# Spatial gate of a small convolutional transformer with its pixels on partitions, gates by tanh, and three tail products

## The chip, the cores and the metric

The kernel runs on one core of one Trainium2 chip. The metric is the device time of one execution in microseconds (us). Three executions of the kernel before took 211.3, 211.53 and 212.07 us; the median is 211.53 us. Engines are called PE (TensorE; PEld are its weight loads), DVE (VectorE), ACT (ScalarE), POOL (GpSimd) and SP (SyncE).

## What is computed

The input is x, float32, 4 images of 64 channels and 16 x 16 pixels. Four layers each add a mixer and then a mixture of eight experts. The change touches the mixer of layer 1 alone. Its reference, cut to what matters (`out` is the sum of a 1x1, a 3x3 and a 5x5 convolution of the normalised input):

```python
avg = jnp.mean(out, axis=(2, 3), keepdims=True)
mx = jnp.max(out, axis=(2, 3), keepdims=True)
ca = jax.nn.sigmoid(ca_mlp(avg) + ca_mlp(mx))                 # one gate per image and channel
c = out * ca
sa_in = jnp.concatenate([jnp.mean(c, axis=1, keepdims=True), jnp.max(c, axis=1, keepdims=True)], axis=1)
sa = jax.nn.sigmoid(conv2d(sa_in, sa_w, pad=3))               # one gate per image and pixel, 7x7
cbam_out = c * sa
...
similarity = jnp.exp(-dist_sq / (2.0 * sigma * sigma))
attn = jax.nn.softmax(similarity, axis=-1)
ao = jnp.einsum('bnm,bcm->bnc', attn, v)
non_local = out + ao.reshape(B, C, H, W)
cat = jnp.concatenate([cbam_out, non_local], axis=1)
return conv2d(cat, tail_w, tail_b)                            # 1x1, 128 -> 64 channels
```

## The kernel before

All data stay in SBUF. A tile has 128 partitions: two images of 64 channels one above the other (`HALVES`), and 512 columns: two parts (`INNER`, the index `j`) of 256 pixels. `chunk(t, j)` is the part j, `tile(t, i)` a piece of 128 columns. Nothing is scheduled by a program: every engine has its own block, the order in it is written out by hand, and the engines wait for each other by semaphores (`S[...]`). PE executes its products in the order of its block.

The mixer of layer 1 on PE (from L531): 25 taps of the convolution (L555) for part 0, then 25 for part 1. Between the taps of part 1 stand the small works of part 0: `queries_keys` (L443), `channel_hidden` and `channel_gates` (L450, L457, the channel gate), `values` (L462), `gated_tokens` (L484: the gated image is transposed, so that a pixel is a partition), `distances` (L472), `spatial_gates` (L490). Behind the taps the same works follow for part 1 (L559 to L574), mixed with `attend` (L508), `spatial_map` (L502), `tail` (L523) and `center` (L293) of the next layer norm. The two engines beside it:

- DVE (L1197 to L1210): `gate_channels(j)` prepares the queries and keys and multiplies by the channel gate; `token_features(j)` (L1164) takes the sum and the maximum over the channels of each pixel, from PSUM; `gate_logits(j)` (L1174) clamps the logits of the pixel gate; `gate_both` (L1179) multiplies by the pixel gate; `normalise` (L1183) divides the attention by its sum and adds the convolution's output `O`; `add_input` (L1192) adds the bias and the layer's input.
- ACT (L814 to L831): for each part it copies the convolution's output, squares queries and keys, applies the exponentials of the attention (`similarities`, L793) and of the gates. A sigmoid is written with Exp, Ln and Exp over a tile of two partitions (one per image) and 256 pixels (`gate_pixels`, L806).

The pixel gate is a product of the features (weights of two columns) with a Toeplitz matrix of the 7x7 kernel (256 moving columns), four times (L497). Its result has an image per partition, and `spatial_map` spreads it to 128 partitions by a product with `to_half`. These are its lines:

```python
last = mm(gate_ps[j][0:2, 0:PIX], sa_feat[:, at:at + 2],
          toeplitz[:, (2 * c + n) * PIX:(2 * c + n + 1) * PIX], ...)
```

Of the kernel before, what the change touches and what calls it, by code (L numbers as in the profile page):

```python
# [27 lines left out]
def pack_plan():  # L28

    plan = {  # L30
        "first": [("center", 128), ("average", 128), ("eps6", 1), ("eps5", 1), ("minus_one", 1), ("one", 1)],
# [21 lines left out]
def metaformer(nc, a):  # L53
# [7 lines left out]
    with ExitStack() as ctx:  # L61
# [24 lines left out]
        to_half = sb("to_half", [2, 128])  # L86
# [24 lines left out]
        def tile(t, i):  # L111
# [4 lines left out]
            borders_zero c_tok ca_cl ca_e ca_h ca_in ca_r ca_s ca_top cbam_done conv_done conv_loaded  # L116
# [7 lines left out]
            route_parts routed route_rows route_shift route_transposed sa_bc sa_cl sa_in sa_map sa_ps small_loaded  # L124
# [37 lines left out]
        O, QK, gated, cbam, ao_n, nonlocal_ = mixer  # L162
# [28 lines left out]
        ca = sb("ca", [128, 4 * INNER])  # L191
        sa = sb("sa", [2, 4 * COLS])
# [30 lines left out]
        SETUP = 8  # L223

# [58 lines left out]
        def _(pe):  # L283
# [173 lines left out]
            def channel_gates(j):  # L457
                pe.wait_ge(S["small_loaded"], 64)
                pe.wait_ge(S["ca_r"], j + 1)
                mm(gate_ps[j][:, 0:1], ca2[0:8, :], ca_in[:, j:j + 1], start=True, stop=True).then_inc(S["ca_s"], 1)  # L460
# [11 lines left out]
            def distances(j):  # L472

                pe.wait_ge(S["qk_lin"], 4 * j + 4)
                pe.wait_ge(S["qk_sq"], 4 * j + 4)
                pe.wait_ge(S["pool_setup"], SETUP)
                for h in range(HALVES):
                    for m in range(2):
# [1126 lines left out]
```

## Time and profile before

| | |
|---|---|
| median of three executions | 211.53 us |
| the profiled execution's own time | 211.5 us |
| its span, first to last instruction | 209.7 us |
| PE busy | 195.9 us (93%), 1112 records |
| DVE busy | 124.5 us (59%) |
| ACT busy | 129.3 us (62%) |
| POOL busy | 42.5 us (20%) |
| granted clock of PE, mean | 1.000 |
| share of the chain that ended last, PE | 78% |

Busy times are sums of the records of an engine; they overlap between engines. An f32 product shows two records on PE and two on PEld. The chain that ended last is followed back from the last instruction, at each step to what released it. The gap between the span and the execution's own time (1.8 us) lies outside of the instructions.

### The profile page before, as it was taken

What the parts mean: (1) busy time and instruction counts of PE and PEld (TensorE: products, weight loads), DVE (VectorE), ACT (ScalarE), POOL (GpSimd) and SP (SyncE); (2) the same over time, 40 slices, a digit from 0 to 9 for tenths busy, and PEclk for the clock granted to TensorE, in tenths of its full rate; (3) what the DMA queues carried; (4) which work ended last, traced back from release to release, by engine and by line L of the source; (5) the groups of instructions that cost most, each with busy time, mean ns of one, the idle gap of its engine ahead of it and who ended that gap; (6) DMA issues with size and microseconds to landing.
All of it is one profiled execution on the core that took longest, in us unless ns stands there. A gap on an engine that the chain in (4) does not pass through costs nothing.

```text
span 209.7 us, 3083 instructions
## 1 busy us (share of the span) xinstructions
PE 195.9 (93%) x1112; PEld 91.5 (44%) x1120; DVE 124.5 (59%) x364; ACT 129.3 (62%) x216; POOL 42.5 (20%) x60
## 2 busy tenths in 40 slices
PE   7998999999999998999999999999998997799993
PEld 2654222348876764322222363532234594333221
DVE  0466879957641824945342547595455688586435
ACT  2535688646355683776575830688685675598682
POOL 7761000000000000103963000100920011010740
PEclk9999999999999999999999999999999999999999
DMA  6999300000000000000000000000000000000001
GB/s 228 355 407 404 123 0 2 0 0 3 2 3 0 3 0 0 0 5 0 0 0 0 0 3 0 0 0 0 0 6 0 2 0 3 0 0 0 3 0 50
DMA packets 3119, 8.40 MB, mean 40 GB/s; under 512 B 550, under 2 KB 1072, under 8 KB 2976
## 3 DMA queue, kind: packets, MB, share of 16 engines
q1 hardware_dynamic: 2736, 7.60, 9.7%
q0 software_dynamic: 224, 0.46, 0.6%
q8 instruction: 9, 0.15, 0.3%
q10 hardware_dynamic: 144, 0.13, 0.2%
q14 instruction: 6, 0.05, 0.1%
HBM read 7.94 MB, written 0.26 MB: 39 GB/s over the span
## 4 chain that ended last, share of the span: by engine, by line
PE 78%; DVE 10%; ACT 8%; issue 3%; DVEq 0%; ACTq 0%
PE bank L362 17%; PE banks L379 9%; PE banks L291 8%; PE banks L380 7%; PE banks L555 6%; PE bank L302 5%; PE bank L296 4%; ACT hidden L727 3%; PE bank L343 3%; PE banks L516 2%; PE banks L497 2%; PE bank L612 2%; PE bank L480 2%; PE bank L325 2%; ACT rstd L689 1%
## 5 line engine op out<-in xcount | busy, mean ns | idle before, releaser
L727 ACT ACTIVATE hidden<-banks,pack_l 128x1024 f32<-128x1024 f32 (+1 forms) x43 | 44.9, 1052 | 18.3 <-PE banks L380 17.8
L362 PE MATMUL bank<-hidden,w 128*64 128x512 f32 (+1 forms) x160 | 41.4, 596 | 1.3 <-ACT hidden L727 1.3
L291 PE MATMUL banks<-idle_work 128*128 128x512 bf16 x116 | 31.1, 401 | 2.0 <-DVE idle_work L1000 1.2
L379 PE MATMUL banks<-split_x,w_hi 128*128 128x512 f16 x80 | 30.7, 384 | 0.0
L380 PE MATMUL banks<-split_x,w_lo 128*128 128x512 f16 x80 | 30.3, 379 | 0.0
L1442 POOL CAST split_x<-normed 64x256 f16<-64x256 f32 x8 | 4.0, 494 | 99.7 <-DVE normed L896 95.2
L685 ACT ACTIVATE squares<-bank 128x256 f32<-128x256 f32 x18 | 6.9, 383 | 22.5 <-PE bank L296 22.4
L379 PEld LDWEIGHTS banks<-split_x,w_hi 128*128 128x128 f16 x80 | 7.7, 97 | 28.4 <-issue 11.5
L291 PEld LDWEIGHTS banks<-idle_work 128*128 128x128 bf16 x123 | 12.4, 105 | 16.2 <-issue 5.0
L1451 POOL TENSOR_TENSOR total<-total,term 128x512 f32<-128x512 f32 x12 | 17.6, 1463 | 2.6 <-DVE term L982 2.0
L362 PEld LDWEIGHTS bank<-hidden,w 128*64 128x64 f32 x160 | 7.9, 134 | 18.3 <-issue 13.6
L896 DVE TENSOR_TENSOR normed<-bank,rstd 128x256 f32<-128x256 f32 x16 | 6.7, 424 | 12.8 <-ACT rstd L689 12.7
L982 DVE TENSOR_TENSOR term<-relu_sim,bank 128x512 f32<-128x512 f32 x12 | 7.8, 685 | 9.5 <-PE bank L343 6.1
L555 PE MATMUL banks<-padded,conv_hi 128*64 128x256 f16 x100 | 12.0, 280 | 0.1
L555 PE MATMUL banks<-padded,conv_lo 128*64 128x256 f16 x100 | 11.9, 277 | 0.0
L302 PE MATMUL bank<-squares,pack_first 128*128 128x256 f32 x36 | 11.3, 414 | 0.4
L736 ACT ACTIVATE relu_sim<-bank,pack_l 128x512 f32<-128x512 f32 x16 | 10.9, 682 | 1.0 <-PE bank L362 0.8
L982 DVE TENSOR_TENSOR term<-sq_sim,bank 128x512 f32<-128x512 f32 x6 | 4.1, 687 | 11.9 <-ACT sq_sim L736 6.8
L296 PE MATMUL bank<-x,pack_first 128*128 128x256 f32 x28 | 9.1, 419 | 1.7 <-DVE x L998 0.7
L1451 POOL TENSOR_TENSOR total<-x,term 128x512 f32<-128x512 f32 x3 | 3.8, 1270 | 33.3 <-DVE term L982 33.3
L689 ACT ACTIVATE rstd<-bank,pack_first 128x256 f32<-128x256 f32 x18 | 8.3, 472 | 3.1 <-PE bank L302 2.8
L380 PEld LDWEIGHTS banks<-split_x,w_lo 128*128 128x128 f16 x80 | 7.8, 98 | 4.7
(314 smaller groups left out, 322.3 us busy)
## 6 DMA issues: line engine op xcount, KB each, us to landing
w_stage<-in_w SPq DMA_DIRECT2D x3, 512.0 KB, 13.2
w_stage<-in_w SPq DMA_DIRECT2D x1, 1024.0 KB, 9.6
conv<-in_conv SPq DMA_DIRECT2D x1, 800.0 KB, 7.7
w<-in_w SPq DMA_DIRECT2D x3, 256.0 KB, 13.4
w<-in_w SPq DMA_DIRECT2D x1, 512.0 KB, 10.4
toeplitz<-in_toeplitz SPq DMA_DIRECT2D x1, 512.0 KB, 11.2
gauss<-in_gauss SPq DMA_DIRECT2D x1, 512.0 KB, 12.4
pack_l<-in_pack_l SPq DMA_DIRECT2D x1, 373.5 KB, 14.9
```

Source lines behind the costliest of these rows:

```text
L291: mm(out, idle_work[:, 0:128], idle_work[:, 0:cols], start=True, stop=True)
L296: mm(bank[4 + j][:, 0:PIX], P("first", "center"), chunk(src, j), start=True, stop=True)\
L302: mm(bank[6 + j][:, 0:PIX], P("first", "average"), chunk(squares, j), start=True, stop=True)\
L362: last = mm(out[64 * h:64 * h + 64, cut], w2[l][:, (f * NE + e) * CH:(f * NE + e + 1) * CH], hidden[v % 3][:, h * 512 + cut.start:h * 512 ...
L379: mm(out, w1_hi[l][:, at:at + 128], split_x[h][:, :], start=True, stop=False)
L380: last = mm(out, w1_lo[l][:, at:at + 128], split_x[h][:, :], start=False, stop=True)
L555: last = mm(image(conv_ps[j][64 * h:64 * h + 64, 0:PIX]), w[:, t * CH:(t + 1) * CH], pads[h][:, j, dy:dy + SIDE, dx:dx + SIDE], start=t == ...
L689: act(chunk(rstd, j), bank[6 + j][:, 0:PIX], ACT.Abs_reciprocal_sqrt, bias=P("first", "eps6" if LN_EPS[k] == 1e-6 else "eps5")).then_inc(S ...
L727: last = act(hidden[u % 3][:, cut], both[u % 2][:, cut], ACT.Gelu, bias=P(f"l{l}", "e_b1")[:, e * fc + f:e * fc + f + 1])
L736: act(y_sb[e], bank[4 + e % 2][:, :], ACT.Identity, bias=P(f"l{l}", "e_b2")[:, e:e + 1])\
L982: TT(out[:, :], y_sb[e], bank[6 + e % 2][:, :], ALU.mult).then_inc(S["moe_term"], 1)
L1451: G.tensor_tensor(total[:, :], (total if e else x[2 * l + 1])[:, :], term[e % 3][:, :], ALU.add)\
```

## The change

It does these things, all in the mixer of layer 1:

- The product of the pixel gate is turned: the Toeplitz matrix gives the weights (128 x 128) and the features are the moving operand (two columns), eight times per part. The logits then have a pixel per partition, 128 x 4 in all.
- The mean over the channels comes from PE: `gated_tokens` gets a product with a column of `average` beside each transpose; the DVE copies four columns instead of summing and scaling.
- Both sigmoids are written as 0.5 tanh(x/2) + 0.5, with one ACT pass (on 128 x 1 and on 128 x 4); the DVE's clamps go. `widen_gates` writes each pixel's gate 64 times, and `spatial_map` transposes this with two products with the identity. The set of ACT's tables that is loaded ahead is another one.
- `normalise` no longer adds `O`; the tail has a third product, of `tail1` with `O`.
- The order: `distances` ahead of `gated_tokens` (and with a wait per image), `values(1)` ahead of `channel_hidden(1)`, `attend(1)` and `spatial_map(1)` ahead of `tail(0)`, `center(4, 0)` directly behind `tail(0)`; on the DVE `token_features(1)` behind `gate_both(0)` and `normalise(0)`, and `add_input(0)` behind `gate_both(1)`.
- The constants `to_half` and `one` go, with the DMA of `to_half`.

```diff
             def gated_tokens(j):
                 pe.wait_ge(S["gated_c"], j + 1)
                 for m in range(2):
-                    last = tr(tile(gate_ps[j], m), tile(gated, 2 * j + m), P("l0", "identity"))
+                    tr(tile(gate_ps[j], m), tile(gated, 2 * j + m), P("l0", "identity"))
+                    last = mm(gate_ps[j][:, MEANS + 2 * m:MEANS + 2 * m + 2], tile(gated, 2 * j + m),
+                              P("first", "average")[:, 0:65:64], start=True, stop=True)
                 last.then_inc(S["c_tok"], 1)
 
             def spatial_gates(j):
                 pe.wait_ge(S["toeplitz_loaded"], 16)
                 pe.wait_ge(S["sa_in"], 2 * j + 2)
-                for c in range(2):
-                    for n in range(2):
-                        at = 8 * j + 4 * c + 2 * n
-                        last = mm(gate_ps[j][0:2, 0:PIX], sa_feat[:, at:at + 2],
-                                  toeplitz[:, (2 * c + n) * PIX:(2 * c + n + 1) * PIX],
-                                  start=c + n == 0, stop=c + n == 2)
+                for o in range(2):
+                    for c in range(2):
+                        for n in range(2):
+                            at, to = 8 * j + 4 * c + 2 * n, (2 * c + n) * PIX + o * 128
+                            last = mm(gate_ps[j][:, LOGITS + 2 * o:LOGITS + 2 * o + 2], toeplitz[:, to:to + 128],
+                                      sa_feat[:, at:at + 2], start=c + n == 0, stop=c + n == 2)
                 last.then_inc(S["sa_ps"], 1)
 
             def spatial_map(j):
-                pe.wait_ge(S["sa_map"], j + 1)
-                mm(gate_ps[j][:, 0:PIX], to_half[:, :], sa[:, 4 * PIX * j + 3 * PIX:4 * PIX * (j + 1)],
-                   start=True, stop=True).then_inc(S["sa_bc"], 1)
+                pe.wait_ge(S["sa_wide"], j + 1)
+                for o in range(2):
+                    last = mm(tile(gate_ps[j], o), tile(sa_wide, 2 * j + o), P("l0", "identity"), start=True, stop=True)
+                last.then_inc(S["sa_bc"], 1)
...
-                pairs = [("tail0", "cbam_done", cbam), ("tail1", "nonlocal_in", nonlocal_)]
-                for n, (weight, ready, src) in enumerate(pairs if j == 0 else pairs[::-1]):
+                parts_ = [("tail1", "conv_out", O), ("tail0", "cbam_done", cbam), ("tail1", "nonlocal_in", ao_n)]
+                for n, (weight, ready, src) in enumerate(parts_):
                     pe.wait_ge(S[ready], j + 1)
-                    last = mm(tail_ps[j][:, 0:PIX], P("l1", weight), chunk(src, j), start=n == 0, stop=n == 1)
+                    last = mm(tail_ps[j][:, 0:PIX], P("l1", weight), chunk(src, j), start=n == 0, stop=n == 2)
...
             queries_keys(1)
+            values(1)
             channel_hidden(1)
             spatial_map(0)
             channel_gates(1)
             attend(0, range(2, 4))
-            values(1)
+            distances(1)
             gated_tokens(1)
-            distances(1)
             spatial_gates(1)
+            attend(1)
+            spatial_map(1)
             tail(0)
-            attend(1)
             center(4, 0, x[3], x_ready(3))
-            spatial_map(1)
             tail(1)
...
             def gate_pixels(j):
-                part = [sa[:, (4 * j + n) * PIX:(4 * j + n + 1) * PIX] for n in range(4)]
-                sc.wait_ge(S["sa_cl"], j + 1)
-                st.link(act(part[1], part[0], ACT.Exp, scale=-1.0))
-                st.link(act(part[2], part[1], ACT.Ln, bias=P("first", "one")[0:2, :]))
-                act(part[3], part[2], ACT.Exp, scale=-1.0).then_inc(S["sa_map"], 1)
+                sc.wait_ge(S["sa_ps"], j + 1)
+                tanh_half(sa_tanh[:, 4 * j:4 * j + 4], gate_ps[j][:, LOGITS:LOGITS + 4]).then_inc(S["sa_map"], 1)
...
                 by_group = gate_ps[j][:, 0:PIX].rearrange("p (g c) -> p g c", c=64)
-                summed = st.mark(rsum(sa_feat[:, 8 * j:8 * j + 4], by_group))
+                V.tensor_copy(sa_feat[:, 8 * j:8 * j + 4], gate_ps[j][:, MEANS:MEANS + 4]).then_inc(S["sa_in"], 1)
                 rmax(sa_feat[:, 8 * j + 4:8 * j + 8], by_group).then_inc(S["sa_in"], 1)
-                ve.wait_ge(st.sem, summed)
-                TS(sa_feat[:, 8 * j:8 * j + 4], sa_feat[:, 8 * j:8 * j + 4], 1.0 / CH, None, ALU.mult)\
-                    .then_inc(S["sa_in"], 1)
...
+            def widen_gates(j):
+                ve.wait_ge(S["sa_map"], j + 1)
+                TS(chunk(sa_wide, j).rearrange("p (g c) -> p g c", c=64), spread_to(sa_tanh[:, 4 * j:4 * j + 4], 64),
+                   0.5, 0.5, ALU.mult, ALU.add).then_inc(S["sa_wide"], 1)
...
-                st.link(TT(chunk(ao_n, j).rearrange("p (r c) -> p r c", c=64), got[:, :, 0:64], spread_to(iz, 64),
-                           ALU.mult))
-                TT(chunk(nonlocal_, j), chunk(ao_n, j), chunk(O, j), ALU.add).then_inc(S["nonlocal_in"], 1)
+                TT(chunk(ao_n, j).rearrange("p (r c) -> p r c", c=64), got[:, :, 0:64], spread_to(iz, 64), ALU.mult)\
+                    .then_inc(S["nonlocal_in"], 1)
```

How the order moves, at three places. First PE behind the second half of attention 0, that is the distances, the transposes and the pixel gate of part 1. `mixer` stands for `O`, `gated`, `cbam` and the like, `R` and `L` are the operands of the distances, `banks` are PSUM. Before:

```order
L469 MATMUL banks<-pack_l,mixer 128x128 [waits v_rows]
L469 MATMUL banks<-pack_l,mixer 128x128
L487 MATMUL banks<-pack_l,mixer 128x128 [waits gated_c]
L487 MATMUL banks<-pack_l,mixer 128x128
L480 MATMUL bank<-R,L 128x256 [waits pool_setup,qk_sq,qk_lin]
L480 MATMUL bank<-R,L 128x256 x3
L497 MATMUL banks<-toeplitz,sa_feat 2x256 [waits sa_in,toeplitz_loaded]
L497 MATMUL banks<-toeplitz,sa_feat 2x256 x3
```

After the change:

```order
L481 MATMUL bank<-R,L 128x256 [waits qk_sq,qk_lin,pool_setup]
L481 MATMUL bank<-R,L 128x256
L481 MATMUL bank<-R,L 128x256 [waits qk_sq,qk_lin]
L481 MATMUL bank<-R,L 128x256
L489 MATMUL banks<-pack_l,mixer 128x128 [waits gated_c]
L490 MATMUL banks<-pack_first,mixer 128x2
L489 MATMUL banks<-pack_l,mixer 128x128
L490 MATMUL banks<-pack_first,mixer 128x2
L502 MATMUL banks<-sa_feat,toeplitz 128x2 [waits sa_in,toeplitz_loaded]
L502 MATMUL banks<-sa_feat,toeplitz 128x2 x7
```

The distances stand ahead of the transposes now, the values have gone to an earlier place, two products of two columns came in, and the gates follow the transposes directly.

Second, PE from there to the last `center` of the stage (L296, L297 in the changed kernel). Before:

```order
L528 MATMUL banks<-mixer,pack_l 128x256 [waits cbam_done]
L528 MATMUL banks<-mixer,pack_l 128x256 [waits nonlocal_in]
L516 MATMUL banks<-v_rows,sq_sim 64x65 [waits attn,v_rows]
L516 MATMUL banks<-v_rows,sq_sim 64x65 x15
L296 MATMUL bank<-x,pack_first 128x256 [waits x_ready]
L505 MATMUL banks<-sa,to_half 128x256 [waits sa_map]
L528 MATMUL bank<-mixer,pack_l 128x256 [waits nonlocal_in]
L528 MATMUL bank<-mixer,pack_l 128x256 [waits cbam_done]
L296 MATMUL bank<-x,pack_first 128x256 [waits x_ready]
```

After the change:

```order
L521 MATMUL banks<-v_rows,sq_sim 64x65 [waits attn,v_rows]
L521 MATMUL banks<-v_rows,sq_sim 64x65 x15
L510 MATMUL banks<-pack_l,mixer 128x128 [waits sa_wide]
L510 MATMUL banks<-pack_l,mixer 128x128
L533 MATMUL banks<-mixer,pack_l 128x256 [waits conv_out]
L533 MATMUL banks<-mixer,pack_l 128x256 [waits cbam_done]
L533 MATMUL banks<-mixer,pack_l 128x256 [waits nonlocal_in]
L297 MATMUL bank<-x,pack_first 128x256 [waits x_ready]
L533 MATMUL bank<-mixer,pack_l 128x256 [waits conv_out]
L533 MATMUL bank<-mixer,pack_l 128x256 [waits cbam_done]
L533 MATMUL bank<-mixer,pack_l 128x256 [waits nonlocal_in]
L297 MATMUL bank<-x,pack_first 128x256 [waits x_ready]
```

Attention 1 and the map of the pixel gate went ahead of both tails; a center stands directly behind the tail that it waits for, and the second tail behind that center.

Third, the DVE from the value rows of part 1 (L1160, L1157) to the first addition of the input (L1194, L1187). Before:

```order
L1160 TENSOR_TENSOR v_rows<-banks,pack_l 128x4x64 [waits v_rows_ps]
L892 TENSOR_REDUCE sa_feat<-banks 128x4 [waits c_tok]
L889 TENSOR_REDUCE sa_feat<-banks 128x4
L1171 TENSOR_SCALAR sa_feat<-sa_feat 128x4 [waits dve_chain]
L1181 TENSOR_TENSOR mixer<-banks,mixer 128x256 [waits sa_bc]
L1187 RECIPROCAL inv_z<-banks 128x4 [waits ao_ps]
L1188 TENSOR_TENSOR mixer<-banks,inv_z 128x256 [waits dve_chain]
L1190 TENSOR_TENSOR mixer<-mixer 128x256 [waits dve_chain]
L1176 TENSOR_SCALAR sa<-banks 2x256 [waits sa_ps]
L1194 SCALAR_TENSOR_TENSOR x<-banks,pack_l,x 128x256 [waits tail]
```

After the change:

```order
L1157 TENSOR_TENSOR v_rows<-banks,pack_l 128x4x64 [waits v_rows_ps]
L1175 TENSOR_TENSOR mixer<-banks,mixer 128x256 [waits sa_bc]
L1181 RECIPROCAL inv_z<-banks 128x4 [waits ao_ps]
L1182 TENSOR_TENSOR mixer<-banks,inv_z 128x256 [waits dve_chain]
L1165 COPY sa_feat<-banks 128x4 [waits c_tok]
L890 TENSOR_REDUCE sa_feat<-banks 128x4
L1170 TENSOR_SCALAR mixer<-sa_tanh 128x256 [waits sa_map]
L1181 RECIPROCAL inv_z<-banks 128x4 [waits ao_ps]
L1182 TENSOR_TENSOR mixer<-banks,inv_z 128x256 [waits dve_chain]
L1175 TENSOR_TENSOR mixer<-banks,mixer 128x256 [waits sa_bc]
L1187 SCALAR_TENSOR_TENSOR x<-banks,pack_l,x 128x256 [waits tail]
```

The features of part 1 (from `c_tok`) come behind the gate and the attention of part 0, and the input is added last.

## Rows read from the trace of the kernel before

**Rows 1.** The page, its span and first part, and the cores' granted clock

```profile
span 209.7 us, 3083 instructions
PE 195.9 (93%) x1112; PEld 91.5 (44%) x1120; DVE 124.5 (59%) x364; ACT 129.3 (62%) x216; POOL 42.5 (20%) x60
core 0: 209.7 us, clock 1.000
```

**Rows 2.** Busy time by stretch, from the last tap to the end of the tails

```profile
66.50:72.80 6.30, 6.30 (x60) 4.96 (x56) 4.58 (x19) 3.67 (x10) 0.00 (x0) 1.00 0.00 0
72.80:80.30 7.50, 7.50 (x53) 4.46 (x52) 2.89 (x8) 4.93 (x9) 0.00 (x0) 1.00 0.01 2
```

Columns: stretch, its length, then busy us and records of PE, PEld, DVE, ACT and POOL, granted clock, DMA share, GB/s.

**Rows 3.** Timeline of PE: start, us from start to end, line, operands, idle before

```profile
70.73 0.44 PE L487 MATMUL banks<-pack_l,mixer 128*128 128x128 f32 x2
...
74.64 1.13 PE L528 MATMUL banks<-mixer,pack_l 128*128 128x256 f32 x4
75.70 2.14 PE L516 MATMUL banks<-v_rows,sq_sim 128*64 128x65 f32 x32
77.77 0.70 PE L296 MATMUL bank<-x,pack_first 128*128 128x256 f32 x2
78.40 0.69 PE L505 MATMUL banks<-sa,to_half 2*128 2x256 f32 x2
79.04 1.27 PE L528 MATMUL bank<-mixer,pack_l 128*128 128x256 f32 x4
80.89 0.70 PE L296 MATMUL bank<-x,pack_first 128*128 128x256 f32 x2 [0.58 <-DVE x L1194]
```

**Rows 4.** Timeline of ACT, exponentials of attention 1 and gate of part 1

```profile
73.52 1.32 ACT L804 ACTIVATE sq_sim<-relu_sim,pack_first 128x512 f32<-128x512 f32 x2
75.20 0.42 ACT L810 ACTIVATE sa<-sa 2x256 f32<-2x256 f32 x1 [0.36 <-DVE sa L1176]
...
76.19 0.42 ACT L812 ACTIVATE sa<-sa 2x256 f32<-2x256 f32 x1
```

**Rows 5.** Timeline of PE's weight loads behind the last tap

```profile
67.38 0.23 PEld L447 LDWEIGHTS bank<-mixer,pack_l 128*64 128x64 f32 x4
67.99 0.10 PEld L454 LDWEIGHTS banks<-stats,pack_l 128*8 128x8 f32 x2 [0.39 <-DVE stats L1140]
...
70.89 1.60 PEld L480 LDWEIGHTS bank<-R,L 96*128 96x128 f32 x8
72.82 1.38 PEld L497 LDWEIGHTS banks<-toeplitz,sa_feat 128*2 128x2 f32 x8 [0.33 <-issue]
74.64 0.73 PEld L528 LDWEIGHTS banks<-mixer,pack_l 128*128 128x128 f32 x4 [0.44 <-issue]
...
79.04 0.30 PEld L528 LDWEIGHTS bank<-mixer,pack_l 128*128 128x128 f32 x2 [0.35 <-DVE mixer L1190]
79.61 0.30 PEld L528 LDWEIGHTS bank<-mixer,pack_l 128*128 128x128 f32 x2 [0.27 <-DVE mixer L1181]
```

**Rows 6.** Weight loads and small products of other shapes: timeline, and single lines (ns min/median/max)

```profile
83.78 0.97 PEld L325 LDWEIGHTS bank<-pack_l,normed 128*128 128x128 f32 x8 [0.66 <-DVE normed L896]
...
L325 PEld LDWEIGHTS bank<-pack_l,normed x24: 186/192/192, 83.8 to 185.3; 128*128 128x128 f32 x24
...
75.70 2.00 PEld L516 LDWEIGHTS banks<-v_rows,sq_sim 128*64 128x64 f32 x32 [0.33 <-issue]
...
L593 PE MATMUL bank<-bn,pack_l x2: 251/262/272, 129.8 to 129.9; 128*128 128x2 f32 x2
```

**Rows 7.** Timeline of DVE: features of part 1, and the last addition

```profile
71.20 0.42 DVE L892 TENSOR_REDUCE sa_feat<-banks 128x4 f32<-128x256 f32 x1
71.54 0.41 DVE L889 TENSOR_REDUCE sa_feat<-banks 128x4 f32<-128x256 f32 x1
71.88 0.16 DVE L1171 TENSOR_SCALAR sa_feat<-sa_feat 128x4 f32<-128x4 f32 x1
...
80.35 0.48 DVE L1194 SCALAR_TENSOR_TENSOR x<-bank,pack_l,x 128x256 f32<-128x256 f32 x1 [0.79 <-PE bank L528]
```

More of the change, by code:

```diff
@@ L30, in pack_plan @@
     plan = {
-        "first": [("center", 128), ("average", 128), ("eps6", 1), ("eps5", 1), ("minus_one", 1), ("one", 1)],
+        "first": [("center", 128), ("average", 128), ("eps6", 1), ("eps5", 1), ("minus_one", 1)],
         "l0": [("identity", 128), ("W", 128), ("b_row", 64), ("router", 16), ("router_b", 8), ("e_b1", 8),
@@ L161, in metaformer @@
         qnorm, rnorm, unit, t_rows = mixer[0:4]
-        O, QK, gated, cbam, ao_n, nonlocal_ = mixer
+        O, QK, gated, cbam, ao_n, sa_wide = mixer
         upsampled, bn_in, bn_relu = mixer[0:3]
@@ L190, in metaformer @@
         ca_in = sb("ca_in", [8, 2])
-        ca = sb("ca", [128, 4 * INNER])
-        sa = sb("sa", [2, 4 * COLS])
+        ca = sb("ca", [128, 2 * INNER])
+        sa_tanh = sb("sa_tanh", [128, 4 * INNER])
         sa_feat = sb("sa_feat", [128, 16])
@@ L223, in metaformer @@
         SETUP = 8
+        MEANS, LOGITS = 256, 264
         ROOTS, LOGS = "abs_reciprocal_sqrt_and_small", "natural_log_exp_and_others"
@@ L457, in channel_gates @@
             def channel_gates(j):
-                pe.wait_ge(S["small_loaded"], 64)
+                pe.wait_ge(S["small_loaded"], 48)
                 pe.wait_ge(S["ca_r"], j + 1)
@@ L547, in _ @@
                         if t == 13:
+                            distances(0)
                             gated_tokens(0)
-                            distances(0)
                         if t == 17:
@@ L1136, in gate_channels @@
                 mean, top = stats[:, 2 * j:2 * j + 1], stats[:, 2 * j + 1:2 * j + 2]
-                gate = [ca[:, 4 * j + n:4 * j + n + 1] for n in range(4)]
                 ve.wait_ge(S["conv_out"], j + 1)
@@ L1149, in gate_channels @@
                         .then_inc(S["qk_lin"], 1)
-                    if h == 0:
-                        ve.wait_ge(S["ca_s"], j + 1)
-                        TS(gate[0], gate_ps[j][:, 0:1], -80.0, None, ALU.max).then_inc(S["ca_cl"], 1)
                 ve.wait_ge(S["ca_e"], j + 1)
-                st.link(TS(gate[2], gate[1], 1.0, None, ALU.add))
-                st.link(V.reciprocal(gate[3], gate[2]))
-                TS(chunk(gated, j), chunk(O, j), gate[3], None, ALU.mult).then_inc(S["gated_c"], 1)
+                tanh, gate = ca[:, 2 * j:2 * j + 1], ca[:, 2 * j + 1:2 * j + 2]
+                st.link(TS(gate, tanh, 0.5, 0.5, ALU.mult, ALU.add))
+                TS(chunk(gated, j), chunk(O, j), gate, None, ALU.mult).then_inc(S["gated_c"], 1)
             def value_rows(j):
@@ L1199, in _ @@
             token_features(0)
-            gate_logits(0)
+            widen_gates(0)
             gate_channels(1)
             value_rows(1)
-            token_features(1)
             gate_both(0)
             normalise(0)
-            gate_logits(1)
-            add_input(0)
+            token_features(1)
+            widen_gates(1)
             normalise(1)
             gate_both(1)
+            add_input(0)
             add_input(1)
@@ L1532 @@
     vals["first"] = {"center": eye - avg, "average": avg, "eps6": np.full((128, 1), 1e-6), "eps5": np.full((128, 1), 1e-5),
-                     "minus_one": np.full((128, 1), -1.0), "one": np.ones((128, 1))}
+                     "minus_one": np.full((128, 1), -1.0)}
     vals["l0"] = {"identity": eye, "W": _both_halves(v["L0_conv_W"].T), "b_row": _row(v["L0_conv_b"]),
```

22 lines of the change are left out of this document (7 added, 15 removed).

## The prediction

> **What bounds the kernel now.** I read the page first: one core, TensorE busy 93% of 209.7 us, its granted clock 1.000 (the 2.4 GHz level) throughout [rows 1]. The other engines have room, so the question is whether TensorE leads in the stage that changes too. The busy time by stretch answers it: between 66.5 us and 80.3 us, the part of the layer-1 mixer behind the convolutions, PE is busy for all of 6.30 and of 7.50 us, while VectorE and ScalarE are busy for 4.58 and 3.67 us, then for 2.89 and 4.93 us [rows 2]. TensorE runs in program order, so a product queued ahead of the last `center(4, 1)` moves everything behind it.
>
> The timeline of PE at the end of the stage has hardly a hole: gates of the pixels (L497), tail 0, attention 1, `center(4, 0)`, pixel map 1, tail 1; only then 0.58 us idle until VectorE has added the input, and `center(4, 1)` starts at 80.89 us [rows 3]. ScalarE's chain for the pixel gate of batch part 1 ends at 76.19 + 0.42 = 76.61 us [rows 4], and PE takes its result (L505) only at 78.40 us [rows 3]. That chain, which the change shortens, is 1.8 us off the path. What the change adds to PE is on it.
>
> **How PE spends a group.** The weight loads show the pace [rows 5]. Four f32 products with 256 moving columns take 72.82 - 70.89 = 1.93 us (L480), two take 75.70 - 74.64 = 1.06 us [rows 3], one takes 78.40 - 77.77 = 0.63 us [rows 3]: 0.43 us for each further product, 0.63 us for the last of a group. Each f32 product is two records. With 128 weight columns and few moving ones (L325, 16 columns) eight loads take 0.97 us, each lasting 0.19: (0.97 - 0.19) / 7 = 0.111 us from one record to the next [rows 6]. That is the price of the new small products.
>
> **The change, part by part.**
>
> 1. `gated_tokens` gets two products for the channel means beside its two transposes: 2 x 2 records x 0.111 = 0.44 us. It runs for both batch parts, on PE, nothing beside it: **+0.88**. VectorE loses a sum of 0.42 us and a scaling of 0.16 us and gains a small copy, which PE doesn't see for part 0 (four taps of the convolution stand between).
>
> 2. `spatial_gates` now loads the Toeplitz blocks as weights and moves two columns: 8 products, 16 records x 0.111 = 1.78 us, against 74.64 - 72.82 = 1.82 us now (L497) [rows 5]. **0**. I take the row of L325 because its weights have the same shape; both bounds stand in the rivals.
>
> 3. `spatial_map` becomes two products of 128 columns (4 records, 0.44 us and the end of a group) for one of 256 (0.63 us): **0**.
>
> 4. `tail` gets a third product, 0.43 us, in both parts: **+0.86**. The sum on VectorE that it replaces (0.42 us each) isn't on PE's path: in tail 0 it was long done, in tail 1 part of a wait, see 7.
>
> 5. New wait, `spatial_gates(1)`: before, `distances(1)` (1.93 us) stood between the transposes and the gates and covered VectorE's reductions. Now `distances(1)` comes ahead of the transposes and nothing is between. A small product lasts 0.262 us (L593) [rows 6], 0.15 more than the 0.111 to the next record; then 0.03 to VectorE's start (71.17 to 71.20), 0.16 for the copy (nearest row L1171), 0.41 for the maximum [rows 7], 0.06 back to PE (80.83 to 80.89): **+0.81**. Behind it are queued attention 1 and both tails. The cover that moved doesn't help anyone: attention 1 waits for ScalarE's exponentials, whose 1.32 us end at 74.84 [rows 4], before PE asks for them either way.
>
> 6. New wait, `center(4, 0)`: now attention 1 stands between tail 0 and this center. In the new order tail 0 is directly ahead of it, and tail 1 is queued behind. The last rows of the stage show the price: load of the last tail product 79.61, VectorE's addition 80.35 to 80.83, center 80.89 [rows 3, 5, 7], 1.28 us from load to load where an unhindered group takes 0.63: **+0.65**.
>
> 7. Given back: the small product of the channel gate waits for VectorE's mean (load at 67.99, 0.61 us behind the last, where 0.45 is the pace of that group) [rows 5]; now `values(1)` fills it: **-0.15**. Tail 1's second product comes 79.61 - 79.04 = 0.57 us after the first because of the pixel gate's product on VectorE [rows 5]; that is done early now: 0.43, **-0.14**.
>
> 8. The three ScalarE passes for the pixel gate (0.42 each or more) [rows 4] become one small tanh, VectorE's clamps go, one tiny DMA goes, and the table load of the stage is exchanged for one of another set. None of it is on the path, for PE asks later: **0**. If PE did wait there, this would be worth 1.1 us per part (third rival).
>
> Sum: 0.88 + 0.86 + 0.81 + 0.65 - 0.29 = **+2.9 us**. The profiled execution took 211.5 us (span 209.7), the median is 211.53, so the two stand together and the sum carries over: **214.4 us**, 1.4% more. The layers behind are unchanged and only shift. About 0.5% (1.06 us) is what a measurement here can tell from no change.
>
> **Rivals.**
>
> *Cheap weight loads.* The 40 records of the small products (32 in the gates, 8 for the means) could cost less than 0.111 us, if the next load runs fully under the product before it. For it: attention's loads of 64 columns follow each other in (2.00 - 0.217) / 31 = 0.0575 us [rows 3, 5, 6]. Against it: L325 has the very shape and shows 0.111. At 0.0575 the sum loses 40 x 0.0535 = 2.1 us: 212.3. At nothing at all it loses 4.4: 210.0. So it ends between faster and the same. Its point of decision is the record pitch of the gates' products: below some 0.063 us the change reads as none.
> The Trainium skill ("TensorE: Matmul & The Clock Gate", section "Back-to-back issue gap") has a table by which a product with up to 64 moving columns follows in about 60 cycles; at 2.4 GHz that would make 1.0 us of the 40 records, an estimate, and 211.0 us of the whole. By the row of L325 the table doesn't hold where every product brings new f32 weights.
>
> *Products that accumulate wait for each other.* The gates' eight products add into the same two columns. If each of the 32 records had to end (0.262 us) before the next, that is 32 x 0.151 = 4.8 us more: 219.2. No row shows so small an accumulating product; L497's, 256 wide, don't wait.
>
> *The pixel gate's chain is the bound after all.* Then taking two ScalarE passes and the clamp out saves some 1.1 us per part and the added products run under other waits: 211.5 - 2.2 = 209.3, **faster**. It decides only if the map of part 1 were ready after 78.40 us; it is ready at 76.61 [rows 3, 4].
>
> *The two new waits cost little,* because PE preloads weights and VectorE answers faster than its rows: without 5 and 6 the time is 213.0, still slower. PE can't go around a waiting product, which speaks against it.
>
> **How the numbers follow.** The forecast as summed 0.71; cheap loads 0.12 (0.03 of it faster, 0.09 the same); accumulation 0.04; chain as the bound 0.03; cheap waits 0.10. The forecast's own lower tail gives 0.02 to "the same". Faster 0.03 + 0.03 = 0.06; the same 0.11; slower 0.69 + 0.04 + 0.10 = 0.83. The range leaves out the accumulation above and most of the first and third rival below: 212.3 (the loads at 0.0575) to 216.0 (each of the four terms a third to a half larger: 2.9 x 1.5 = 4.4). The forecast's own range is 213.4 to 215.6.
>
> **What would show it.** In the profile after: the gates' eight products in about 1.8 us; two small ones of 0.44 us beside the transposes; three tail products in 1.5 us; PE idle by some 0.8 us ahead of the gates of part 1, released by VectorE's maximum, and by some 0.6 us ahead of `center(4, 0)`; `center(4, 1)` at about 83.8 us in place of 80.89, and the same distance from there to the end. It is wrong if that start comes before 82, if the gates take under 1 us or over 3, or if PE waits for the wide gates.

## The result, and the profile after

The changed kernel takes 215.08 us (median of four executions, 214.51 to 216.01) against 211.42 us for the kernel before beside it (211.07 to 212.07): the ratio is 1.0177, 95% interval 1.015 to 1.0203. It is slower by 3.7 us, where the prediction said 2.9 (214.4 us, range 212.3 to 216.0). The profiled execution took 214.51 us.

The first lines of its page, which answer to [rows 1], with the granted clock of the 40 slices of the span:

```profile
span 212.7 us, 3144 instructions
PE 198.6 (93%) x1152; PEld 97.1 (46%) x1152; DVE 122.2 (57%) x356; ACT 126.9 (60%) x212; POOL 42.0 (20%) x59
PEclk9999999999999969999999999999999999999999
```

DVE and ACT each lost 2.3 to 2.4 us of work, PE gained 2.7, and the time followed PE. What is new is in the third line: one slice at 0.6. The kernel before had the clock at its upper level all through.

The timeline of PE in the last part of the stage, which answers to [rows 3]:

```profile
68.69 0.71 PE L510 MATMUL banks<-pack_l,mixer 128*128 128x128 f32 x4
...
72.58 0.27 PE L489 MATMUL banks<-pack_l,mixer 128*128 128x128 f32 x1
72.69 0.28 PE L490 MATMUL banks<-pack_first,mixer 128*128 128x2 f32 x2
72.83 0.31 PE L489 MATMUL banks<-pack_l,mixer 128*128 128x128 f32 x1
72.97 0.28 PE L490 MATMUL banks<-pack_first,mixer 128*128 128x2 f32 x2
73.93 1.92 PE L502 MATMUL banks<-sa_feat,toeplitz 128*128 128x2 f32 x16 [0.68 <-DVE sa_feat L890]
75.78 2.19 PE L521 MATMUL banks<-v_rows,sq_sim 128*64 128x65 f32 x32
77.89 1.22 PE L510 MATMUL banks<-pack_l,mixer 128*128 128x128 f32 x4
78.91 1.87 PE L533 MATMUL banks<-mixer,pack_l 128*128 128x256 f32 x6
81.36 0.70 PE L297 MATMUL bank<-x,pack_first 128*128 128x256 f32 x2 [0.58 <-DVE x L1187]
81.89 1.46 PE L533 MATMUL bank<-mixer,pack_l 128*128 128x256 f32 x6
83.93 0.70 PE L297 MATMUL bank<-x,pack_first 128*128 128x256 f32 x2 [0.58 <-DVE x L1187]
```

Both new waits are there: 0.68 us ahead of the gates (L502), released by the maximum, and 0.58 us ahead of `center(4, 0)` (L297). Then compare like with like: the four records of L510 (map 1, two products) take 1.22 us; the same four for part 0, in the first line, take 0.71. The tail behind them, six records, lasts 1.87 us, the second tail with the same six lasts 1.46. The stretches of the stage say why (columns as in [rows 2]; the third from the right is the granted clock):

```profile
75.00:76.00 1.00, 1.00 (x12) 0.98 (x12) 0.00 (x0) 0.12 (x1) 0.00 (x0) 1.00 0.00 0
76.00:77.00 1.00, 1.00 (x20) 1.00 (x20) 0.29 (x1) 0.98 (x2) 0.00 (x0) 0.66 0.00 0
77.00:78.00 1.00, 1.00 (x18) 0.88 (x15) 0.00 (x0) 0.36 (x1) 0.00 (x0) 0.50 0.00 0
78.00:79.00 1.00, 1.00 (x5) 1.00 (x6) 0.61 (x2) 0.00 (x0) 0.00 (x0) 0.50 0.00 0
79.00:80.00 1.00, 1.00 (x5) 0.81 (x5) 0.42 (x1) 0.00 (x0) 0.00 (x0) 0.64 0.00 0
80.00:81.00 1.00, 0.78 (x4) 0.35 (x2) 0.18 (x1) 0.00 (x0) 0.00 (x0) 1.00 0.00 0
```

Between 76 and 80 us the clock goes down to its lower level, 1.2 GHz (0.50), and comes back. Before it fell, PE had waited, had run the 16 records of two columns and was in the attention. The busy share of PE doesn't show it: it is 1.00.

The weight loads, which answer to [rows 5]:

```profile
67.31 0.23 PEld L448 LDWEIGHTS bank<-mixer,pack_l 128*64 128x64 f32 x4
67.92 0.52 PEld L470 LDWEIGHTS banks<-pack_l,mixer 128*128 128x128 f32 x4 [0.39 <-issue]
...
72.83 0.34 PEld L490 LDWEIGHTS banks<-pack_first,mixer 128*128 128x128 f32 x2
73.90 1.86 PEld L502 LDWEIGHTS banks<-sa_feat,toeplitz 128*128 128x128 f32 x16 [0.73 <-issue]
75.78 2.00 PEld L521 LDWEIGHTS banks<-v_rows,sq_sim 128*64 128x64 f32 x32
```

(1.86 - 0.19) / 15 = 0.111 us per record: the pace that [rows 6] gave for another line. The gates take 75.78 - 73.90 = 1.88 us against 1.82 before (L497).

**The stage.** One number serves for all comparisons below: from the first weight load of `queries_keys(0)` to the first load of the last `center(4, 1)`. Before it is 80.89 - 55.33 = 25.56 us, after 83.93 - 54.86 = 29.07 us. The 3.51 us between them are nearly the whole 3.7 us; the stage merely began 0.47 us earlier in this execution. Each stage time below comes from one profiled execution, and the times in us are medians. The start of the stage lies between 54.58 and 55.84 us in the profiles of this document, whatever the kernel, so that the stage resolves more than the whole time does.

### The profile page after: what moved, and what is told of

It is laid out like the page before. It is cut to its first block, busy times and chain, and to the rows that moved or that the text cites. A ratio compares the mean times of both kernels' runs of the same rounds, so it can differ in the third digit from the quotient of the medians.

```text
span 212.7 us, 3144 instructions
## 1 busy us (share of the span) xinstructions
PE 198.6 (93%) x1152; PEld 97.1 (46%) x1152; DVE 122.2 (57%) x356; ACT 126.9 (60%) x212; POOL 42.0 (20%) x59
## 4 chain that ended last, share of the span: by engine, by line
PE 78%; DVE 11%; ACT 7%; issue 3%; DVEq 0%; ACTq 0%
PE bank L363 17%; PE banks L380 9%; PE banks L292 7%; PE banks L381 7%; PE banks L560 6%; PE bank L303 5%; PE bank L297 4%; ACT hidden L732 3%; PE bank L344 3%; PE banks L521 2%; PE bank L481 2%; PE banks L502 2%; PE bank L617 2%; PE bank L326 2%; ACT rstd L694 1%
## 5 line engine op out<-in xcount | busy, mean ns | idle before, releaser
L292 PE MATMUL banks<-idle_work 128*128 128x512 bf16 x123 | 32.0, 396 | 1.2 <-DVE idle_work L1001 1.2
L292 PEld LDWEIGHTS banks<-idle_work 128*128 128x128 bf16 x123 | 12.3, 105 | 16.0 <-issue 4.7
L297 PE MATMUL bank<-x,pack_first 128*128 128x256 f32 x28 | 9.1, 419 | 2.3 <-DVE x L1187 1.2
```

The costliest lines, as they stand in the source:

```text
L292: mm(out, idle_work[:, 0:128], idle_work[:, 0:cols], start=True, stop=True)
L297: mm(bank[4 + j][:, 0:PIX], P("first", "center"), chunk(src, j), start=True, stop=True)\
```

## The experiments

The theory was that waits and added products sum on PE, and, once the trace was seen, that the clock's fall adds to it. The questions: do the waits go when the order is repaired; what lets the clock fall; what is each part of the arithmetic worth.

**e1: the distances between the transposes and the gates.**

```diff
-            distances(1)
             gated_tokens(1)
+            distances(1)
             spatial_gates(1)
```

> The changed kernel with distances(1) back between gated_tokens(1) and spatial_gates(1), nothing else. 'Stage' is the time from the first weight load of queries_keys(0) to the first load of the last center(4, 1): 25.56 us before, 29.07 us after the change. Theory (waits and products add up, clock fell because PE was idle in the wait): the 0.68 us of idle time ahead of the gates of part 1 goes, and so does the stretch at a granted clock of 0.50: stage 27.6 to 27.8, about 1.4 us less than the changed kernel. Rival (the clock falls because the small products move two columns only, the wait has nothing to do with it): the wait goes, the stretch at 0.50 stays, stage 28.4, 0.7 us less. Second rival (the wait only moves, since the distances now delay the attention's exponentials): stage above 28.8.

Measured: 215.09 us, stage 84.49 - 55.31 = 29.18 us, nothing gained. Its timeline of PE, then its stretches:

```profile
73.76 1.84 PE L502 MATMUL banks<-sa_feat,toeplitz 128*128 128x2 f32 x16
76.01 2.19 PE L521 MATMUL banks<-v_rows,sq_sim 128*64 128x65 f32 x32 [0.41 <-ACT sq_sim L809]
78.13 1.22 PE L510 MATMUL banks<-pack_l,mixer 128*128 128x128 f32 x4
79.14 2.20 PE L533 MATMUL banks<-mixer,pack_l 128*128 128x256 f32 x6
```

```profile
77.00:78.00 1.00, 1.00 (x20) 1.00 (x18) 0.00 (x0) 0.23 (x1) 0.00 (x0) 0.61 0.00 0
78.00:79.00 1.00, 1.00 (x8) 0.88 (x6) 0.61 (x2) 0.00 (x0) 0.00 (x0) 0.50 0.00 0
```

The second rival holds: the wait ahead of the gates is gone (PE's loads wait 0.23 us for VectorE ahead of the transposes in its place), and the attention (L521) waits 0.41 us for ScalarE's exponentials instead, since the distances come later and tail 0 is no longer between. The clock falls all the same.

**e2: tail 0 ahead of attention 1.** The two lines of PE's order below, `spatial_map(1)` behind `center(4, 0)`, and `add_input(0)` ahead of `normalise(1)` on VectorE.

```diff
             spatial_gates(1)
+            tail(0)
             attend(1)
-            spatial_map(1)
-            tail(0)
             center(4, 0, x[3], x_ready(3))
+            spatial_map(1)
             tail(1)
```

> The changed kernel with tail(0) ahead of attend(1) and add_input(0) ahead of normalise(1) again, center(4, 0) and then spatial_map(1) behind attend(1); distances(1) stays ahead of gated_tokens(1). The wait of center(4, 0) goes (0.58 us of idle PE, 0.65 by the price of the prediction). Theory: stage 28.4 if the stretch at 0.50 stays. If the 256-wide products of tail 0 between the small products and the attention keep the clock up, another 0.7 less: 27.7. Rival (center(4, 0)'s wait was hidden): no change, 29.1.

Measured: 214.38 us, stage 83.81 - 55.41 = 28.40 us, 0.67 less than the changed kernel. The wait of `center(4, 0)` is gone, and the clock still falls:

```profile
78.00:79.00 1.00, 1.00 (x18) 1.00 (x18) 0.49 (x1) 0.00 (x0) 0.00 (x0) 0.50 0.00 0
```

The 0.67 us are near the price of that wait (0.65), but they are a net of several things: the low clock lies over the attention for the most part, which hardly feels it, and tail 1 now waits 0.48 us in its loads for VectorE's product with the gate. A cleaner reading of the same wait follows with e8.

**e3: both orders.**

> Both orders of the two runs before together: only the arithmetic of the change is left, in the old order apart from values(1) ahead of channel_hidden(1). Theory: both waits gone and the clock at 1.00: 29.07 - 0.7 - 0.65 - 0.7 = 27.0 for the stage; what is left over the kernel before, 1.4 to 1.6 us, is the 0.88 us of the mean products and the 0.86 us of the third tail products, less 0.15 to 0.3. Rival (the clock falls from the small products alone): 27.7. Rival (the added products are cheap and the waits were all of it): 25.6 to 26.

Measured: 213.30 us, stage 82.56 - 55.50 = 27.06 us, 2.0 less than the changed kernel. The timeline of PE has hardly any idle time but the last (the stretches have 0.09 us from 71 to 72 and 0.08 from 80 to 81):

```profile
73.95 1.84 PE L502 MATMUL banks<-sa_feat,toeplitz 128*128 128x2 f32 x16
75.65 1.54 PE L533 MATMUL banks<-mixer,pack_l 128*128 128x256 f32 x6
77.12 2.14 PE L521 MATMUL banks<-v_rows,sq_sim 128*64 128x65 f32 x32
79.19 0.70 PE L297 MATMUL bank<-x,pack_first 128*128 128x256 f32 x2
...
82.56 0.70 PE L297 MATMUL bank<-x,pack_first 128*128 128x256 f32 x2 [0.58 <-DVE x L1187]
```

The granted clock is 1.00 in every stretch of the stage. The order, with the fall of the clock that goes away with it, is worth 2.0 us of the 3.5; 1.5 us stay with the arithmetic.

**e4: the wait filled with products of zeros.**

```diff
             gated_tokens(1)
+            busy(3, bank[5][:, :])
             spatial_gates(1)
```

> The changed kernel with three products of zeros, 128 x 512 bf16 (0.22 us each by the rows of L291), ahead of spatial_gates(1), where PE waited for the features; no result depends on them. The wait stays in length, but PE is busy in it. Theory (the idle time made the clock fall): granted clock 1.00 throughout, stage 28.4, 0.7 us less than the changed kernel, though PE does more. Rival (the small products alone make it fall): the stretch at 0.50 stays, and the stage is 29.0 to 29.2. If the filling products run past the end of the wait, up to 0.2 us more in either case.

Measured: 215.37 us, stage 84.72 - 55.39 = 29.33 us. PE works through the wait (L292), and the clock falls none the less (0.69 from 77 to 78 us, 0.50 until 80):

```profile
73.64 0.81 PE L292 MATMUL bank<-idle_work 128*128 128x512 bf16 x3
...
79.44 2.13 PE L533 MATMUL banks<-mixer,pack_l 128*128 128x256 f32 x6
```

```profile
78.00:79.00 1.00, 1.00 (x12) 0.88 (x9) 0.43 (x2) 0.00 (x0) 0.00 (x0) 0.50 0.00 0
```

The idle time is not what it takes; the theory as I put it falls here, its rival holds. The filling is of zeros; whether other numbers would act alike is not shown.

**e8: the small products made wide.** The gates' products move 128 columns, the same two repeated, in the order and with the waits of the changed kernel.

```diff
-  last = mm(gate_ps[j][:, LOGITS + 2 * o:LOGITS + 2 * o + 2], toeplitz[:, to:to + 128],
-            sa_feat[:, at:at + 2], start=c + n == 0, stop=c + n == 2)
+  last = mm(gate_ps[j][:, MEANS + 128 * o:MEANS + 128 * o + 128], toeplitz[:, to:to + 128],
+            repeat(sa_feat[:, at:at + 2], 64), start=c + n == 0, stop=c + n == 2)
```

> The changed kernel, order and waits as they are, with each of the gates' small products moving 128 columns in place of 2 (the same two columns of features, repeated 64 times by the access pattern). The weight loads set their pace, 0.111 us a record, and a record of 128 moving columns takes no longer, so the gates still take 1.88 us. Theory (the clock falls because these products move almost nothing for 1.9 us, next to the wait and the attention): granted clock 1.00 throughout the stage, stage 28.4, 0.7 us less than the changed kernel, 214.4 us. Rival (the waits alone, or attention 1 alone, make it fall): the stretch at 0.50 stays, stage 29.1. Rival (the moving columns cost time of their own beside the loads): gates over 2.5 us each, stage over 29.5.

Measured: stage 83.94 - 55.59 = 28.35 us, 0.72 less than the changed kernel, clock 1.00 in all of it:

```profile
74.76 2.02 PE L502 MATMUL banks<-sa_feat,toeplitz 128*128 128x128 f32 x16 [0.68 <-DVE sa_feat L892]
76.72 2.14 PE L521 MATMUL banks<-v_rows,sq_sim 128*64 128x65 f32 x32
78.78 0.71 PE L510 MATMUL banks<-pack_l,mixer 128*128 128x128 f32 x4
79.33 1.46 PE L533 MATMUL banks<-mixer,pack_l 128*128 128x256 f32 x6
```

The same wait, the same attention, 64 times the moving columns, and the map and the tail are back at 0.71 and 1.46 us. Compare L510 to `center(4, 0)`: 81.37 - 78.78 = 2.59 us here, 81.36 - 77.89 = 3.47 us in the changed kernel. The low clock cost 0.88 us there; the slower gates (1.99 against 1.88 us, and 1.98 against 1.88 for part 0) took 0.2 back. This run also gives the wait of `center(4, 0)` at the upper clock: from the first load of tail 0 to the center 81.37 - 79.22 = 2.15 us, where e3, whose tail 0 has the attention behind it, takes 77.12 - 75.63 = 1.49: 0.66.

The whole time, though, was 215.52 us, no less than the changed kernel's: three of four executions had a mean clock of 0.992, as all four of the changed kernel have. In the profiled one the clock fell in layer 3, behind a stretch in which PE was busy for only 0.67 of 2 us:

```profile
181.00:183.00 2.00, 0.67 (x2) 0.30 (x2) 1.83 (x7) 1.76 (x2) 0.00 (x0) 1.00 0.00 0
183.00:185.00 2.00, 1.62 (x4) 1.00 (x4) 1.26 (x4) 0.00 (x0) 0.00 (x0) 0.64 0.00 0
185.00:187.00 2.00, 2.00 (x6) 1.37 (x6) 0.00 (x0) 0.77 (x2) 0.00 (x0) 0.51 0.00 0
```

That stretch is no reason by itself: the changed kernel has it too, with the same products and the same idle times ahead of them (0.78 and 0.98 us), and keeps its clock there:

```profile
181.00:183.00 2.00, 0.67 (x2) 0.30 (x2) 1.80 (x7) 1.72 (x2) 0.00 (x0) 1.00 0.00 0
183.00:185.00 2.00, 1.60 (x6) 0.89 (x6) 1.25 (x3) 0.38 (x1) 0.00 (x0) 1.00 0.00 0
```

From the last center to the end of the span e8 takes 213.8 - 83.94 = 129.9 us, the changed kernel 212.7 - 83.93 = 128.8: the fall there cost 1.1 us, more than the other one gave back. The one execution with a mean clock of 1.000 took 213.57 us. So two executions of e8 are known to have had no fall in the mixer; where the clock fell in the two others isn't known.

**e11: e1 with the wide products**, as a second test of the same cause in another order (the diffs of e1 and e8 together).

> e1_dist_between (stage 29.18 us, with a stretch at a granted clock of 0.50) with the gates' products moving 128 columns in place of 2, as in e8_wide_moving. Theory (the small products are what lets the clock fall): clock 1.00 in the mixer, stage 28.4 to 28.5, 0.7 us less than e1. Rival (e8's clock stayed up by chance, since the wait and the attention are as quiet as they were): the stretch at 0.50 is there again, stage 29.1 to 29.3.

Measured: stage 83.25 - 55.22 = 28.03 us, 1.15 less than e1, clock 1.00 in the mixer. More than expected, as e1's low clock lay over more of its tail (2.20 us against 1.46). The time was 214.89 us, again with a fall in layer 3 in the profile. Of the three other executions two had a mean clock of 0.992; one, at 0.998, took 214.67 us, no less than the rest.

**e5: two products in the tail**, on top of e3: VectorE adds `O` again.

```diff
-  parts_ = [("tail1", "conv_out", O), ("tail0", "cbam_done", cbam), ("tail1", "nonlocal_in", ao_n)]
+  parts_ = [("tail0", "cbam_done", cbam), ("tail1", "nonlocal_in", ao_n)]
...
+  TT(chunk(ao_n, j), chunk(ao_n, j), chunk(O, j), ALU.add).then_inc(S["nonlocal_in"], 1)
```

> e3_both (stage 27.06 us, 213.3 us) with the tail of two products again: VectorE adds the convolution's output in normalise as in the kernel before. Theory: 0.43 us of PE per part, stage 26.2 (0.86 less). Rival (the third product fills a wait, because the tail of part 1 waits for the pixel gate's product on VectorE between its second and third anyway, by 0.79 against 0.43 us): only the 0.43 us of part 0 come back and the addition of 0.42 us on VectorE delays that product, stage 26.6 to 27.0.

Measured: 213.11 us, stage 82.39 - 55.77 = 26.62 us, 0.44 less than e3: the rival. Only part 0 gives its 0.43 us back. In part 1 the tail waits for the pixel gate's product on VectorE, which now comes behind one more addition; PE's loads of that tail wait 0.70 us, and from the first load of map 1 to the last center both runs take 3.04 us.

**e6: sums over the channels on VectorE**, on top of e3: the two products with `average` go, the sum and the scaling come back.

> e3_both (stage 27.06 us, 213.3 us) without the mean products: VectorE sums over the channels and scales, as in the kernel before. Theory: each pair of small products costs 0.44 us of PE with nothing beside it, stage 26.2 (0.88 less); the features are ready in time, since distances(1) (1.9 us) covers VectorE's 0.9 us. Rival (small products cost less than the load pace says, since they run between the transposes): 0.5 us less or under, stage 26.5 to 26.9. In e3_both attention 1 also waited for ScalarE's exponentials by no more than 0.1 us; these start with the distances, which now come 0.44 us earlier, so that they don't bind.

Measured: 212.87 us, stage 82.31 - 55.84 = 26.47 us, 0.59 less. The transposes and the way to the distances take 0.17 us (71.58 to 71.75) where e3 took 0.56 (71.55 to 72.11): 0.39 us for the two small products of a part. With 0.34 for part 0 (below) that is 0.73, not 0.88, and some of it went into a short wait ahead of the gates (PE's loads pause 0.25 us), since VectorE's longer features come behind `gate_both(0)` and `normalise(0)`.

**e7: e5 and e6 together.**

> e5 and e6 together: of the change only the turned pixel gate, the tanh and values(1) ahead of channel_hidden(1) are left, in the order of the kernel before otherwise. Theory (the pixel gate with pixels on partitions costs PE nothing and gains nothing): stage 25.3 to 25.6 against 25.56 before, 211.2 to 211.5 us, no difference that can be told. Rival (the shorter chain of the gate is worth its 1.1 us per part): below 25.0 and below 210.5 us. Rival (the turned gate costs PE time of its own): above 25.9.

Measured: 213.74 us, stage 82.04 - 54.74 = 27.30 us: outside of the theory. The timeline of PE shows two waits and a low clock (1.22 us for L297):

```profile
70.76 1.89 PE L481 MATMUL bank<-R,L 96*128 96x256 f32 x8
72.99 1.92 PE L500 MATMUL banks<-sa_feat,toeplitz 128*128 128x2 f32 x16 [0.34 <-DVE sa_feat L1166]
...
77.93 1.22 PE L297 MATMUL bank<-x,pack_first 128*128 128x256 f32 x2
78.94 0.87 PE L508 MATMUL banks<-pack_l,mixer 128*128 128x128 f32 x4
80.33 1.13 PE L531 MATMUL bank<-mixer,pack_l 128*128 128x256 f32 x4 [0.52 <-DVE mixer L1176]
```

With additions and sums back on VectorE, the order that the change gave to VectorE makes the features late. In the profile the clock falls a second time, in layer 3 (0.50 from 182 to 184 us). Three of its ten executions had a mean clock of 1.000, that is neither fall, and took 212.65 to 212.86 us; the seven others, at 0.984, took 213.56 to 214.43. Even without the falls this order is not as fast as the kernel before.

**e9: the turned gate and the tanh in the old order.** As e7, but `token_features(1)` ahead of `gate_both(0)`, `values(1)` in its old place, tail 1 taking the attention first, and `spatial_map(1)` ahead of `center(4, 0)`.

> e7 with the rest of the old order restored: VectorE's features of part 1 ahead of gate_both(0) and normalise(0), values(1) ahead of gated_tokens(1) and not ahead of channel_hidden(1), tail 1 taking the attention's product first; and spatial_map(1) ahead of center(4, 0), so that the gate's product on VectorE is done in time. Of the change only the turned pixel gate and the tanh are left. Theory (this part alone costs and gains nothing on PE): no wait ahead of the gates, stage 25.3 to 25.6 us against 25.56 before, the time within 0.5% of the kernel before, granted clock 1.00 in the stage, since tail 0 stands between the gates and the attention and nothing waits. Rival (the shorter chain of the gate pays): below 25.0. Rival (e7's 27.3 us came from the turned gate itself and not from its order): above 26.

Measured: 211.25 us against 211.69 (ratio 0.9998, interval 0.9968 to 1.0027), stage 80.43 - 55.18 = 25.25 us, clock 1.00 in it, 0.05 us under what was expected. The turned gate with tanh is neutral: 0.3 us less than before in the stage, about half of it from the early map (next run), and nothing that the timing can tell.

**e10: the kernel before with the early map.**

```diff
             attend(1)
-            center(4, 0, x[3], x_ready(3))
             spatial_map(1)
+            center(4, 0, x[3], x_ready(3))
             tail(1)
```

> The kernel before with spatial_map(1) ahead of center(4, 0), nothing else: none of the change's arithmetic. Theory: tail 1's second product no longer waits for VectorE (0.57 against 0.43 us), stage 25.42, 0.14 us less, which no timing can tell: 211.2 to 211.5. Rival (the attention's addition on VectorE now delays tail 1's first product as much): 25.56 to 25.7.

Measured: 211.38 us (ratio 0.9996, interval 0.9967 to 1.0024), stage 80.00 - 54.58 = 25.42 us, as expected to the hundredth. No version here beats the kernel before by anything that can be measured.

| kernel | stage, us | clock in the stage | time, us |
|---|---|---|---|
| before | 25.56 | 1.00 | 211.42 to 211.69 |
| changed | 29.07 | falls | 215.08 |
| e1 distances between | 29.18 | falls | 215.09 |
| e4 wait filled | 29.33 | falls | 215.37 |
| e2 tail 0 early | 28.40 | falls | 214.38 |
| e8 wide gates | 28.35 | 1.00 | 215.52 |
| e11 e1 with wide gates | 28.03 | 1.00 | 214.89 |
| e7 gate only, new order on VectorE | 27.30 | falls | 213.74 |
| e3 both orders | 27.06 | 1.00 | 213.30 |
| e5 two tail products | 26.62 | 1.00 | 213.11 |
| e6 sums on VectorE | 26.47 | 1.00 | 212.87 |
| e10 early map alone | 25.42 | 1.00 | 211.38 |
| e9 gate only, old order | 25.25 | 1.00 | 211.25 |

Stage and clock are those of the profiled execution.

## Why the prediction was right, and where it was short

Its way was right: PE leads, in order, and what is added to it is paid. That the last center stands at 83.93 us, where 83.8 was forecast, is luck in part: the stage began 0.47 us early, and from the start before it would be 84.4. Point by point:

1. **Mean products, +0.88.** 0.34 us in part 0 (59.20 to 61.64 us from the first distance load to the next tap, 2.44 us, against 59.67 to 61.77, 2.10) and 0.39 in part 1 (e6 against e3): 0.73.
2. **Turned gates, 0.** 0.06 us per part; the pace of 0.111 us is exact, and "cheap weight loads" fell. So did "products that accumulate wait for each other": 16 records in 1.88 us.
3. **Map, 0.** In part 0 0.64 us (68.69 to 69.33) against 0.55 for L505 (68.12 to 68.67): 0.1 more. In part 1, at the upper clock, 0.44 (e8, 78.78 to 79.22) against 0.64 (78.40 to 79.04): 0.2 less, since the tail behind it now starts with a product that waits for nothing.
4. **Third tail product, +0.86.** In the order of e3 it is worth half of that: e5 gives back 0.44 us for both parts, for in part 1 the product lies in a wait for VectorE that the sum on VectorE makes longer. In the order of the change nothing speaks against the 0.86: the six loads of tail 1 follow each other in 1.27 us without that wait, and tail 0 with the wait of the center takes 2.15 us (e8) where 1.06 + 0.43 + 0.65 = 2.14 were forecast. No run takes the product away in that order.
5. **Wait ahead of the gates, +0.81.** 0.68 us idle, 0.73 in the loads.
6. **Wait of `center(4, 0)`, +0.65.** 0.66 us by e8 against e3; e2's net is 0.67.
7. **Given back, -0.29.** The -0.15 for the channel gate's product did not come, for there was no wait to fill. In both kernels the next load follows `queries_keys(1)` after 0.61 us (67.38 to 67.99 before, 67.31 to 67.92 after, where it is a load of `values(1)`), and the product with the mean takes 0.13 in both (67.99 to 68.12, 68.56 to 68.69). The -0.14 in tail 1 came, and 0.2 more: `center(4, 0)` and tail 1 take 83.93 - 81.36 = 2.57 us, against 0.63 + 1.85 = 2.48 before (78.40 - 77.77 and 80.89 - 79.04) and 2.77 by the sum. Part of that is the center's product, which has a tail behind it that waits for nothing: 0.53 us from start to start (81.36 to 81.89) in place of 0.63.
8. **ScalarE's and VectorE's savings, 0.** ACT's gate of part 1 is one pass of 0.17 us, and the time didn't feel it. The rival "the pixel gate's chain is the bound" is refuted by e9.

The step that failed is one that isn't in the list. The prediction read the clock as 1.000 in the kernel before [rows 1, 2] and carried it over, although in the gates it replaced eight products of 256 moving columns by sixteen of 2 and put those of part 1 beside a wait and the attention. That cost 0.88 us (e8 against the changed kernel). Up to the first load of attention 1, tail 0 left out, the sum said 0.88 + 0.81 - 0.15 = 1.54 us more than before; measured are 20.92 - 19.31 = 1.61 (75.78 - 54.86 after; 75.70 - 55.33 less the 1.06 us of tail 0 before). From there on, the sum said 0.86 + 0.65 - 0.14 = 1.37 us more than before, tail 0 counted on both sides; measured are 8.15 - 6.25 = 1.90 us (83.93 - 75.78 after; 80.89 - 75.70 and the 1.06 us of tail 0 before). Without the clock that would be 1.0, some 0.35 less than the sum: map 1 and `center(4, 0)` with tail 1 took 0.2 less each (3 and 7). The clock's term, put at nothing, was 0.88 too low. The misses partly cancel: the sum is 0.6 us short of the stage (2.9 against 3.51) and 0.8 short of the time (3.7), of which the medians of four executions don't resolve the last 0.15.

Is it the small products that let the clock fall? The profiles bear that out for this kernel: with 128 moving columns and everything else alike it stays up in the mixer, in two orders (e8, e11), as was expected of both before they ran; with two columns it falls where the attention follows directly (changed, e1, e4) or where PE has waited ahead of them (changed, e2, e7); with tail 0 between and no wait it stays up (e3, e5, e6, e9). All twelve executions of the changed kernel, e1 and e4 had a mean clock of 0.992.

It is not shown beyond doubt, for three reasons. Only a profile tells where the clock fell, and there is one of each kernel. Few moving columns are not enough: three of ten executions of e7 had no fall at all. And they are not needed: the kernel before had a mean clock of 0.992 in 1 of 23 executions beside e9 (213.19 us, where the others had a median of 211.68), and of 0.992 or 0.984 in 5 of 25 beside e5 to e8; e3 had 0.992 in 1 of 5, e9 in 4 of 12 and e10, which has none of the change's arithmetic, in 2 of 12. e8 and e11 have one fall per profile like the changed kernel and e1, only in layer 3. So a rival stands: that most executions with these products have a fall, and that the wide ones moved its place and didn't take it away. More profiles of the changed kernel and of e8 would decide it. For the forecast the two come to the same: the fall in the mixer is what the sum had left out.

## What to carry to other kernels

Taking work from engines that wait and giving it to the one that leads makes a kernel slower by just that work; look first at which engine the work comes from and goes to. When a cover is moved away from between a producer and its consumer, price the latency that it hid (here 0.7 us twice), and look whom the cover's new place delays. And don't carry the granted clock over to a version that changes the shapes and the order of PE's products: here the busy share stayed at 1.00 while the clock fell. Look at the whole time, too, before a stage that got faster counts as a gain (e8).

## What was not expected of the hardware

- In the mixer PE's busy share was 1.00 in each stretch in which the clock went down, and three wide products of zeros in the wait ahead (e4) didn't hold it up. With more moving columns in the gates (e8, e11), and with tail 0 behind the gates and no wait ahead (e3), it stayed up.
- The attention's 32 records took 77.89 - 75.78 = 2.11 us with some three quarters of that at the lower clock, and 77.77 - 75.70 = 2.07 us at the upper one [rows 3]. Not every form of product feels the clock: the groups of 128 and 256 columns behind it did (1.22 against 0.71 us, 1.87 against 1.46).
- Sixteen records of f32 products with 128 weight columns take 1.88 us with 2 moving columns (0.118 a record) and, in e8, 76.72 - 74.73 = 1.99 us with 128 (0.124). The wide form is nearly free.
- e4's three filling products cost nothing by themselves: from the first load of the distances to that of the gates it takes 74.43 - 71.27 = 3.16 us, the changed kernel 73.90 - 70.74 = 3.16. The stage grew by 0.26 us behind them, from map 1 to the center (82.15 - 78.42 = 3.73 against 3.47), where more of tail 0 ran at the lower clock (2.13 us against 1.87).
- The same group costs more when the product behind it has to wait for another engine: from load to load the four records of L510 take 0.64 us (68.69 to 69.33) ahead of the channel gate, and 0.44 (e8, 78.78 to 79.22) ahead of a tail that waits for nothing.
